# Routing in batches of 8, 4, 2 and 2 sequences, and a new order of VectorE's and TensorE's work in attention steps 11 to 17

## What is computed

```
h = layernorm(word[x] + pos + type[mask]) * gamma + beta
h = h + attention(layernorm(h)) @ Wo + bo         # 16 heads, q and k normalized, causal
a = layernorm(h)
scores = softmax(a @ gate_w.T)                     # 8 experts
sel = top_k(scores + expert_bias, 2)
order = argsort(sel, stable)                       # tokens grouped by expert
out = h + scatter_add((silu(xe @ w1[e]) * (xe @ w3[e])) @ w2[e])   # xe = token times its score
```

## Time and profile before

| | us |
|---|---|
| time, median of 3 runs (lowest, highest) | 561.75 (560.3, 562.2) |
| time of the profiled execution | 561.48 |
| its span | 559.7 |
| mean granted TensorE clock in it | 0.978 of 2.4 GHz |
| TensorE matmuls busy | 514.3 |
| VectorE, ScalarE, GpSimd busy | 289.0, 258.0, 270.4 |
| attention and routing, to the first expert matmul | 243.8 |
| experts, from there to the end | 315.9 |

### The profile page before, as it was taken

The page is one execution under the profiler, slowest core; times in us unless marked ns, Lnnn a source line. Parts: engine busy times, 40 slices in busy tenths (PEclk is TensorE's granted clock), DMA queues, the critical chain, the costliest instruction groups (busy, mean ns, idle before and its releaser), DMA issues.

```text
span 559.7 us, 12933 instructions
## 1 busy us (share of the span) xinstructions
PE 514.3 (92%) x4251; PEld 431.4 (77%) x4252; DVE 289.0 (52%) x769; ACT 258.0 (46%) x591; POOL 270.4 (48%) x506
## 2 busy tenths in 40 slices
PE   6778999999999996589999999999999999999991
PEld 2345767776777664269999999999999999999980
DVE  3686888888887669832333333333333333333330
ACT  1068889989998882043223333233332233322320
POOL 4587787777764210132444344443444443444432
PEclk9799999999999999789999999999999999999997
DMA  5017611100138552311211222112222112221221
GB/s 162 9 30 273 205 58 51 35 28 28 50 85 270 181 192 72 123 32 29 39 27 30 38 38 38 28 29 38 38 38 33 26 36 38 38 32 28 35 38 19
DMA packets 29482, 36.64 MB, mean 65 GB/s; under 512 B 7792, under 2 KB 23024, under 8 KB 29456
## 3 DMA queue, kind: packets, MB, share of 16 engines
q0 software_dynamic: 8352, 12.76, 13.4%
q1 hardware_dynamic: 19472, 21.07, 11.7%
q10 hardware_dynamic: 1632, 2.50, 1.4%
HBM read 26.81 MB, written 9.50 MB: 65 GB/s over the span
## 4 chain that ended last, share of the span: by engine, by line
PE 77%; DVE 7%; POOL 5%; issue 3%; ACT 3%; DMA 2%; SPq 0%; ACTq 0%; POOLq 0%; DVEq 0%
PE PS L1348 34%; PE PS L1359 18%; PE PS L1099 9%; PE PS L1203 6%; PE PS L1162 2%; PE PS L1297 2%; PE PS L1179 2%; PE PS L1154 2%; PE PS L1107 2%; DMA cols_sb<-head_cols_dram 1%; ACT work L592 1%; DVE front L818 1%; DVE nmax L829 1%; DVE w_sb L820 1%; PE PS L1216 1%
## 5 line engine op out<-in xcount | busy, mean ns | idle before, releaser
L1348 PEld LDWEIGHTS PS<-work,arena 128*128 128x128 f32 x1716 | 197.6, 192 | 3.8 <-ACT work L699 2.0
L1348 PE MATMUL PS<-work,arena 128*128 128x128 f32 x1716 | 198.1, 276 | 1.5 <-ACT work L699 1.5
L705 ACT ACTIVATE work<-PS 128x768 f32<-128x768 f32 x39 | 31.6, 810 | 197.3 <-PE PS L1348 197.3
L1359 PE MATMUL PS<-w_sb,work 128*128 x468 | 107.6, 380 | 0.7 <-DVE x_pair L1074 0.7
L1066 DVE TENSOR_TENSOR work<-work,PS 128x640 f32<-128x640 f32 x39 | 32.0, 822 | 141.0 <-ACT work L705 141.0
L1359 PEld LDWEIGHTS PS<-w_sb,work 128*128 128x128 f32 x468 | 86.1, 191 | 11.0 <-issue 1.1
L539 POOL DMA_INDIRECT out_dram<-x_pair,dst_c x39 | 79.9, 2049 | 22.0 <-POOL dst_c L538 20.5
L592 ACT ACTIVATE work<-PS,nmax 128x128 f32<-128x128 f32 x256 | 72.8, 407 | 4.6 <-DVE nmax L829 4.6
L538 POOL COPY dst_c<-dest_i 128x1 int32 (+1 forms) x39 | 7.1, 181 | 137.2 <-DVE x_pair L1074 134.9
L695 ACT ACTIVATE arena<-w_sb 128x1408 f32 x40 | 55.1, 1377 | 15.1 <-DVE er_i L1042 10.1
L1099 PE MATMUL PS<-ident,work 128*128 128x128 f32 x336 | 55.4, 278 | 2.4 <-ACT work L592 2.2
(11 more groups left out here) (157 smaller groups left out, 611.9 us busy)
## 6 DMA issues: line engine op xcount, KB each, us to landing
w_sb<-w_dram SPq DMA_DIRECT2D x15, 640.0 KB, 5.9
w_sb<-w_dram SPq DMA_DIRECT2D x7, 704.0 KB, 4.7
x_rows<-x SPq DMA_DIRECT2D x16, 128.0 KB, 1.8
out_dram<-arena SPq DMA_DIRECT2D x16, 128.0 KB, 2.0
w_sb<-w_dram SPq DMA_DIRECT2D x15, 64.0 KB, 6.4
w_sb<-w_qkv_dram ACTq DMA_DIRECT2D x1, 768.0 KB, 7.8
w_sb<-w_dram ACTq DMA_DIRECT2D x1, 704.0 KB, 4.2
work<-x_rows,src_c POOLq DMA_INDIRECT x41, 2.8
```

The source lines that it names most:

```text
L1348: last = n.matmul(up_ps[p][:, i, c, :], ws[p][:, k, at:at + P], xT_sb[p][:, k, :], start=(k == 0), stop=(k == DK - 1))
L1359: last = n.matmul(PS[:, 7, 0:D], hT_sb[p][:, i, :], w2_sb[:, bass.ds(e, 1), i, :], start=(i == 0), stop=(i == FK - 1))
```

## The change

The batches become 0 to 7, 8 to 11, 12 and 13, and 14 and 15. The pieces of routing move to other steps, the one-hots to other memory, and the counts of fill matmuls change. rank(0) writes to its own cells of the values' bank. TensorE does x2's transposes of step 15 and the gate's matmuls of steps 15 and up earlier. The diff, cut to its core:

```diff
-WARM_START, WARM_FIRST, WARM_EXPERTS = 32, 14, 18
+WARM_START, WARM_FIRST, WARM_EXPERTS = 32, 14, 16
 QK_BANK, VY_BANK, T_BANK, O_BANK = 4, 5, 6, 7
 GATE_AT = 320
 MAGIC = float(0x5F3759DF)
-BATCH = ((0, 8), (8, 13), (13, 15), (15, 16))
-EARLY_SEQ = 13
+BATCH = ((0, 8), (8, 12), (12, 14), (14, 16))
 BIG = float(3 * 2 ** 29)
 HALF = P / 2 - 0.5
-WARM = dict(scores=3, rows=2, division=3, mix=2, last=3, outputs=3, project=2, norm=10, route=4)
+WARM = dict(scores=3, rows=2, division=1, mix=1, last=2, back=2, project=2, norm=9, gate=4, choice=9, place=5)
...
         v_aug = [v[:, :].rearrange("p (h w) -> p h w", w=HP) for v in (front[:, 1280:1792], v_late)]
-        lanes = front[:, :].bitcast(f16).rearrange("p (c b s) -> p c b s", c=TOPK, s=P)
...
         sq = late[:, 3 * D:5 * D]
-        cells_early = late[:, 3 * D:3 * D + TOPK * EARLY_SEQ * P // 2].bitcast(f16).rearrange("p (c b s) -> p c b s", c=TOPK, s=P)
-        cells_last = v_late[:, 0:TOPK * (B - EARLY_SEQ) * P // 2].bitcast(f16).rearrange("p (c b s) -> p c b s", c=TOPK, s=P)
+        hot0 = ((5 * D, 9 * D), (7 * D, 3 * D))
+        def hot(i, c, s):
+            if s < 8:
+                return late[:, hot0[c][i] + s * P // 2:hot0[c][i] + (s + 1) * P // 2].bitcast(f16)
+            at = (i * 2 + c) * 8 + s - 8
+            return front[:, at * P // 2:(at + 1) * P // 2].bitcast(f16)
+        def lanes(c, s):
+            return hot(0, c, s)
         def cells(c, s):
-            return cells_early[:, c, s, :] if s < EARLY_SEQ else cells_last[:, c, s - EARLY_SEQ, :]
+            return hot(1, c, s)
         x_in = [x_pair[:, p * D:(p + 1) * D] for p in range(2)]
...
         cell_ps = PS[:, 1, 0:P]
+        ranks0 = PS[:, VY_BANK, D:D + 8 * E].rearrange("p (b e) -> p b e", e=E)
...
                 u = t - 2
-                if at_step(t, B):
+                if at_step(t, B - 1):
                     sp.wait_ge(v_done, B)
...
                 if at_step(t, B):
+                    sp.wait_ge(s_done, RG * B)
+                    sp.wait_ge(cells_done, 1)
+                    load_up(sp, E - 1)
                     store_scores(0)
-                if at_step(t, B):
                     store_scores(1)
             attention(sp, step)
...
                     gate_exponentials(0)
-                if at_step(t, B - 2):
+                if at_step(t, B - 3):
                     gate_exponentials(1)
-                if at_step(t, B):
+                if at_step(t, B - 1):
                     gate_exponentials(2)
-                    act.wait_ge(cells_done, 2)
-                    load_up(act, E - 1)
                 if at_step(t, B + 1):
                     gate_exponentials(3)
...
                 v.tensor_tensor(ranked[:, :, s0:s1, :], oneh[:, :, s0:s1, :],
-                                spread(ranks[:, s0:s1, :], 1, TOPK), ALU.mult).then_inc(picked, 1)
+                                spread(ranks0 if b == 0 else ranks[:, s0:s1, :], 1, TOPK), ALU.mult).then_inc(picked, 1)
                 dve.wait_ge(picked, b + 1)
                 link(v.tensor_reduce(rank[:, :, s0:s1], ranked[:, :, s0:s1, :], axis=AX.X, op=ALU.add))
...
                     for s in range(*BATCH[b]):
-                        v.tensor_scalar(lanes[:, c, s, :], iota_lane[:, :], lane[:, c, s:s + 1], token[:, s:s + 1],
+                        v.tensor_scalar(lanes(c, s), iota_lane[:, :], lane[:, c, s:s + 1], token[:, s:s + 1],
                                         ALU.is_equal, ALU.mult)
                         last = v.tensor_scalar(cells(c, s), iota_cell[:, :], key[:, c, s:s + 1], None, ALU.is_equal)
...
                     stats(link, row(3), 1, var_a)
-                if at_step(t, B - 1):
-                    gate_scores(1, link)
                 if at_step(t, B):
-                    one_hots(0, (1,))
+                    one_hots(1, (1,))
                 if at_step(t, B + 1):
-                    gate_scores(2, link)
+                    places(2, link)
                 if valid(t + 4) and valid(t):
                     sum_rows(t + 4, p, half(4))
...
                     normalize(x2[p][:, :], row(u), 2).then_inc(x2_ready, 1)
+                if at_step(t, B - 4):
+                    gate_scores(0, link)
+                    best_two(0, 4, link)
+                if at_step(t, B - 3):
+                    places(0, link)
+                if at_step(t, B - 2):
+                    gate_scores(1, link)
                 if at_step(t, B - 1):
                     dve.wait_ge(qk_ps, B)
-                    places(0, link)
+                    places(1, link)
                 if at_step(t, B):
-                    places(1, link)
+                    gate_scores(2, link)
+                if at_step(t, B + 1):
+                    one_hots(2)
                 if valid(t + 4) and valid(t):
                     centered(t + 4, p)
...
                     squared_sums(t + 2)
-                if at_step(t, B - 1):
+                if at_step(t, B - 2):
                     best_two(*BATCH[1], link)
                     choose(1, link)
                 if at_step(t, B):
-                    one_hots(1)
-                if at_step(t, B + 1):
                     best_two(*BATCH[2], link)
                     choose(2, link)
...
                 if at_step(t, B - 4):
-                    gate_scores(0, link)
-                    best_two(0, 4, link)
-                if at_step(t, B - 3):
                     best_two(4, 8, link)
                     choose(0, link)
+                if at_step(t, B - 3):
+                    gate_shift(1, link)
+                    one_hots(0, (0,))
                 if at_step(t, B - 2):
-                    gate_shift(1, link)
+                    one_hots(0, (1,))
                 if at_step(t, B - 1):
+                    gate_shift(2, link)
                     dve.wait_ge(v_done, B)
                     dve.wait_ge(pv_done, B - 1)
-                    one_hots(0, (0,))
-                if at_step(t, B):
-                    gate_shift(2, link)
+                    one_hots(1, (0,))
                 u = t - 1
                 if valid(u):
...
             gate_shift(3, link)
-            places(2, link)
             gate_scores(3, link)
             best_two(*BATCH[3], link)
             choose(3, link)
-            one_hots(2)
+            places(3, link)
+            one_hots(3)
             dve.wait_ge(rank_done, 4)
             link(v.tensor_scalar(full[:, :], counts, HALF, BIG, ALU.add, ALU.add))
...
                             ALU.subtract, ALU.is_equal).then_inc(select_ready, 1)
-            places(3, link)
-            one_hots(3)
-            link(v.tensor_scalar(full[:, :], full[:, :], -BIG, None, ALU.add))
             dve.wait_ge(cells_done, len(BATCH))
             v.tensor_copy(cell_sb[:, :], cell_ps).then_inc(cells_out, 1)
+            link(v.tensor_scalar(full[:, :], full[:, :], -BIG, None, ALU.add))
             link(v.tensor_tensor(prior[:, :, :], below[:, :, :], spread(full[:, :], 1, E), ALU.mult))
             dve.wait_ge(table_done, 1)
             v.tensor_scalar(src_i[:, :], table, -1.0, 0.0, ALU.add, ALU.max).then_inc(src_ready, 1)
             link(v.tensor_reduce(base[:, :], prior[:, :, :], axis=AX.X, op=ALU.add))
             link(v.tensor_tensor(le8[:, :, :], spread(iota_tile[0:1, :], 2, E), spread(base[0:1, :], 1, NTP), ALU.is_ge))
...
                 if b == 0:
+                    pe.wait_ge(v_ready, B - 2)
+                    n.matmul(ranks0, upper[:, :], chosen[:, s0:s1, :], start=True, stop=False, skip_group_check=True)
+                    for s in range(s0, s1 - 1):
+                        last = n.matmul(ranks0[:, s + 1:s1, :], onesb[:, :], spread(chosen[:, s, :], 1, s1 - s - 1),
+                                        start=False, stop=(s == s1 - 2), skip_group_check=True)
+                    last.then_inc(rank_done, 1)
+                    return
+                if b == 1:
                     pe.wait_ge(qkn_ready, B)
                 else:
                     pe.wait_ge(picked, b)
-                n.matmul(ranks[:, s0:s1, :], upper[:, :], chosen[:, s0:s1, :], start=(b == 0), stop=False,
+                n.matmul(ranks[:, s0:s1, :], upper[:, :], chosen[:, s0:s1, :], start=(b == 1), stop=False,
                          skip_group_check=True)
-                for s in range(s0, s1):
-                    last = n.matmul(ranks[:, s + 1:B + 1, :], onesb[:, :], spread(chosen[:, s, :], 1, B - s),
+                for s in range(0 if b == 1 else s0, s1):
+                    at = max(s + 1, s0)
+                    last = n.matmul(ranks[:, at:B + 1, :], onesb[:, :], spread(chosen[:, s, :], 1, B + 1 - at),
                                     start=False, stop=(s == B - 1), skip_group_check=True)
                 last.then_inc(rank_done, 1)
...
                     for s in range(s0, s1):
-                        last = n.matmul(cell_ps, cells(c, s), lanes[:, c, s, :], start=(b == 0 and c == 0 and s == 0),
```

(36 more changed lines are left out.)

## The result

The changed kernel takes 553.32 us (551.79 to 554.83, 4 runs) against 561.84 (560.3 to 562.2, 4 runs) before: 8.5 us less, a ratio of 0.9876 with a 95% interval of 0.985 to 0.9902. The forecast was 553.4. The profiled execution took 553.11 us.

A forecast was written before the change was run, and what follows sets the result against it. VectorE's routing was taken to bound the start of the first expert matmul. Gains of 5.3 us by the last logits, 1.2 by src_i and 1.85 from the fill make 8.35: 561.75 - 8.35 = 553.4 us, range 551.8 to 556.6.

The forecast's parts named there:

- The stall in step 14: Start of step 14: one-hots at the end of step 13 make the sum, normalize_qk(15) and row maxima 1.5 us late.
- Maxima of step 15: VectorE's row maxima of step 15, behind the second eight pairs of one-hots: start at 204.44 us, 1.36 late.
- outputs(15): TensorE's outputs(15), which waited for VectorE until 214.28 us: now near 213.1, released by ScalarE.
- From there to the sum of step 16: TensorE and VectorE from outputs(15) at 213.1 to the sum at 218.8 us, with 0.75 for reciprocal and product.
- Sum to last logits: From the sum of step 16 to the last logits: stays 4.14 us, with the added work covered; logits at 222.9.
- Tail: Behind the last logits: chosen at 3.03, cell_sb at 6.46, src_i at 7.13 us; 1.2 us gained.
- The fill: TensorE ahead of the experts: sixteen fill matmuls take 3.45 us and end before the gathered block; 1.85 us gained.
- rival 2: Clock falls in the tail (gain 6.9, 554.9 us) or as up(0) begins (gain 5.5, 556.2); chance 0.25.
- rival 3: GpSimd's ten operations of qk_power(15) slowed under the one-hots, 0.26 each, 2.6 us; gain 7.4, 554.3 us; chance 0.12.
- SP's queue: Takes load_up of expert 7 from ScalarE; stores wait behind it, the first gather for these, at least 5 us later.
- Slower: Clock falls at TensorE's idle time in step 14 and stays low until 222 us; 565 us; chance 0.03.
- 11 us: Work leaving VectorE in steps 15 to 17, 6.2 us of it sixteen pairs of one-hots; VectorE ceases to be the bound.

The follow-up runs named there:

- The split: Changed kernel with four of step 13's eight pairs of one-hots moved into VectorE's idle time behind places(0); one run of 551.65 us.
- the load on ScalarE: Changed kernel with load_up of expert 7 issued by ScalarE in step 16 instead of SP; first expert matmul 66.31 us behind the maxima of step 12.
- the run with nine fills: Changed kernel with nine instead of five fill matmuls behind the last rank; first expert matmul 66.35 us behind the maxima of step 12.
- the repeat: Changed kernel again with no edit; 553.29 us, ratio 0.9864 to a kernel before of 560.06 us.
- the one with late one-hots: Changed kernel with batch 0's one-hots back in steps 15 and 16, and batch 1's moved to the middle of step 16; 556.05 us.

## Why the prediction was right, and where it was not

The predicted time and the mechanism were right. Step by step, behind the mark:

- **The stall in step 14**: forecast 1.5 us (the text's own 193.4 makes it 1.42), measured 1.53. The split shows that its cause is the one named.
- **Maxima of step 15**: forecast 1.36 late, measured 1.38.
- **outputs(15)**: forecast at 43.3, measured 43.40, released by ScalarE as forecast.
- **From there to the sum of step 16**: forecast 5.7 us, measured 6.17. The term mis-sized is "reciprocal and product". From the reciprocal to outputs_to_rows it took 1.07 us (215.43 to 216.50) where it had 0.75: the gate's matmuls ahead of outputs_to_rows were left out (0.2 us by the run that moves them). From the projection to the sum it took 1.17 (217.39 to 218.56) instead of 1.0; the rest is hand-overs of under 0.1 us.
- **Sum to last logits**: forecast 4.14, measured 4.12. places(2), four pairs of one-hots and the nine fills were covered.
- **Tail**: forecast chosen at 3.03, cell_sb 6.46, src_i 7.13; measured 3.04, 6.45, 7.10.
- **The fill**: forecast 1.85 us gained behind the block, measured 2.82 less 1.35, or 1.47. The step that failed is the one on the clock: "I take it that the clock holds; it is nearer to the row that held". It fell after 1.54 us of idle time, so the fill ran low and ended last. The price in rival 2 was too high, though. I had the low clock last for 5.5 us of the fill, as before; it lasted some 3.4. The transposes began 0.43 us behind the block, but 0.15 of that is there also where the clock held: with the load on ScalarE it is 1.09 us from the block to the first expert matmul instead of 1.35. So the low clock cost some 0.3 us, not 1.4. What happened is thus the milder form of rival 2 with nearly the result of the forecast. In the run with nine fills its other form came, in the run with the load on ScalarE neither.
- **GpSimd**: its chain for qkn, under the one-hots:

```profile
188.51 0.38 POOL L439 TENSOR_SCALAR nwt<-nwt 128x32 f32<-128x32 f32 x1
...
190.35 0.26 POOL L445 TENSOR_TENSOR rqk<-nwt 128x32 f32<-128x32 f32 x1
```

The two operations took 0.38 and 0.26 us; the ten went from 187.09 to 190.61, 3.5 us against 3.2 before (187.61 to 190.83). The slack hid that, as normalize_qk(15) began only at 192.13, 1.5 us later. It is 0.3 us of the 2.6 that rival 3 would need. The Trainium skill (GPSIMD Engine Reference, Key points) names contention on the SBUF interfaces that the two engines share, with VectorE instructions in a 2-port mode or with two SBUF inputs. No run shows in which mode the one-hots ran, nor tells such contention from other causes. In the split, where the slack is gone, VectorE waits 0.26 us for this chain.
- **SP's queue**: the first gather waited for src_i and its copy and not for SP's stores, and moving the load off the queue left src_i and the block where they were.
- **Slower** never came near: TensorE's idle 1.52 us in step 14 left the clock at 1.0 in the changed kernel.

That the total fits to 0.1 us is partly luck. Of 8.3 us between the two profiled spans, 7.46 are the change and 0.79 the start of the run; I had 8.35 and none. In the repeat the difference of the medians was 6.8 us, and a forecast of 8.35 would have been 1.6 off; by the rows the gain was 0.9 to 1.0 smaller than forecast both times.

Where the 7.46 us come from, by undoing or doing parts alone: the two fills 0.78 (by the kernel before with 16; in the changed kernel they are worth 0.14), the batch sizes 0.05 in themselves, the move of batch 0's one-hots (and with it that of batch 1's) 2.24. The 4.4 that are left are the rest of the new order, TensorE's included, and no run takes it apart in full. The tail's order is 2.5 of it, and up to 1.5 of these are the four pairs of one-hots that left the tail. The parts need not add up exactly, since each was taken against another neighbour. So my account of "11 us" leaving VectorE named the right engine: its busy time from the maxima of step 15 to the last logits fell by 7.8 us (from 23.40 of 25.12 to 15.59 of 19.01), and the stretch by 6.1. By these numbers up to 3.8 us, half of the win, is due to the one-hots that fill the timeline; how much of the other half is due to the small dependent instructions is not shown.

## What to carry to other kernels

When work leaves an engine that bounds a stretch, price the path that takes over and not the work that left: sixteen pairs of 6.2 us were worth 4.0 in the steps they left, and 1.4 of that was paid at once where they stood at the end of a step instead of in a gap. Put moved work into idle stretches in pieces of their size; four pairs shifted by a few instructions gave back 1.3 us. And choose fill matmuls so that they end when the next real work is ready: two too many cost 0.78 us in the kernel before, and where the fill ended 1.2 us too early, the clock fell in the experts in one of two kernels and cost 1.6.

## What the runs showed of the hardware that I had not expected

The granted clock isn't a function of the program alone. The changed kernel and its repeat are one program; in the first 45 us the one had a low stretch between 18 and 22 us, the other two, between 17 and 24 and between 37 and 42. In the tail the clock fell in both, and held in the kernel with the load on ScalarE, whose TensorE has the same orders and the same idle 1.55 us. The length of the idle stretch alone doesn't tell, either: the clock fell 1.1 us behind an idle stretch of 1.54 us, in another kernel behind 1.26 and 0.53 us close together, in the one with late one-hots near 219 us behind 1.46 and 0.47, and it held behind 1.75 us.

The same explains most of the spread between runs, which sits ahead of everything that was changed. The mark came between 167.44 and 170.72 us in fourteen profiles, and it goes with the clock of the first 45 us: with no low stretch there it came at 167.44, with 3.4 us at the low clock at 168.99 and 169.44, with 6.8 us at 169.07 to 170.15, with 10.2 us at 170.04 to 170.72. First the kernel with nine fills, whose mark came first; then the changed kernel's repeat, whose mark came last:

```profile
18.00:20.00 2.00, 2.00 (x7) 0.74 (x6) 1.40 (x4) 0.30 (x1) 0.81 (x2) 1.00 0.22 66
```

```profile
18.00:20.00 2.00, 1.45 (x3) 0.83 (x3) 1.36 (x5) 0.38 (x1) 1.40 (x3) 0.50 0.23 66
...
38.00:40.00 2.00, 2.00 (x6) 1.48 (x7) 1.93 (x4) 0.90 (x3) 2.00 (x4) 0.50 0.00 0
```

The one has the high clock throughout, and its maxima of step 0 start at 32.11 us. The other has two low stretches, and starts them at 34.84. That is 2.7 of the 3.3 us between the two marks. A kernel's time of one run is thus no measure of an edit worth 2 us; a mark inside the profile is.
